# A softplus summed on TensorE instead of VectorE, and four carry columns a slot later, in a convolution and selective-scan kernel

## The reference, cut to what matters

```python
xz = x @ W_in
xh, z = jnp.split(xz, 2, axis=-1)
xh = jax.nn.silu(_causal_conv_k2(xh, conv_w, conv_b))
x_dbl = xh @ W_x
dt_low, Bmat, Cmat = ...                        # 8, 16 and 16 columns
dt = jax.nn.softplus(dt_low @ W_dt + b_dt)      # 256 channels
# per pixel t:  h = exp(dt_t * A) * h + dt_t * B_t * x_t ;  y_t = sum over states (h * C_t)
y = (y + xc * D) * jax.nn.silu(z)
out = y @ W_out
```

## Time and profile before

| | us |
|---|---|
| median of 3 runs (13836.56 to 13845.37) | 13839.43 |
| the profiled execution, its own time | 13837.79 |
| its span, first to last instruction | 13836.0 |
| VectorE busy in it | 13466.6 (97%) |
| GpSimd busy in it | 13246.6 (96%) |
| ScalarE busy in it | 12104.2 (87%) |
| TensorE matmul busy in it | 10079.9 (73%) |

### The profile page before, as it was taken

The page is one execution under the profiler, slowest core; times in us unless marked ns, Lnnn a source line. Parts: engine busy times, 40 slices in busy tenths (PEclk is TensorE's granted clock), DMA queues, the critical chain, the costliest instruction groups (busy, mean ns, idle before and its releaser), DMA issues.

```text
span 13836.0 us, 170380 instructions
## 1 busy us (share of the span) xinstructions
PE 10079.9 (73%) x34752; PEld 2897.7 (21%) x34752; DVE 13466.6 (97%) x12084; ACT 12104.2 (87%) x24809; POOL 13246.6 (96%) x3076
## 2 busy tenths in 40 slices
PE   6777777777777777777777777777777777777776
PEld 1222222222222222222222222222222222222221
DVE  7999999999999999999999999999999999999999
ACT  7888888888888888888988888888898888888888
POOL 6999999999999999999999999999999999999999
PEclk8888888888888888888878888788888888888887
DMA  6667676666766676666667666666666666666665
GB/s 146 161 154 161 155 163 156 158 157 157 164 156 160 152 163 158 160 157 156 158 159 164 153 163 151 163 159 156 161 153 163 156 161 156 160 156 163 158 155 128
DMA packets 1195180, 2175.99 MB, mean 157 GB/s; under 512 B 152321, under 2 KB 161594, under 8 KB 1194042
## 3 DMA queue, kind: packets, MB, share of 16 engines
q1 hardware_dynamic: 1192762, 2164.07, 66.7%
q10 hardware_dynamic: 1280, 0.02, 0.0%
HBM read 1811.17 MB, written 352.32 MB: 156 GB/s over the span
## 4 chain that ended last, share of the span: by engine, by line
POOL 53%; issue 32%; DVE 6%; ACT 5%; PE 1%; DMA 1%; SPq 0%; POOLq 0%; ACTq 0%; DVEq 0%
POOL hq L1064 38%; POOL dbx L1054 15%; DVE hq L946 4%; ACT ps_a L640 2%; DVE dbx L929 1%; ACT dbx L654 1%; DMA b_rep<-bc_d 0%; DMA dt_d<-dt 0%; DVE pp L905 0%; ACT xh L600 0%; ACT L600 0%; ACT L765 0%; PE ps_acc L456 0%; DMA dtx_d<-sp 0%; POOLq L1063 0%
## 5 line engine op out<-in xcount | busy, mean ns | idle before, releaser
L1064 POOL TENSOR_TENSOR hq<-hq,c_rep 128x2048 f32<-128x2048 f32 x2048 | 9251.0, 4535 | 468.8 <-ACT carry L659 465.0
L946 DVE TENSOR_TENSOR_SCAN hq<-ps_a,dbx 128x512 f32<-128x512 f32 x8192 | 9443.6, 1207 | 128.8 <-ACT dbx L654 47.2
L640 ACT ACTIVATE ps_a<-dt_rep,A_neg 128x512 f32<-128x512 f32 x8192 | 5625.2, 687 | 1294.7 <-DVE hq L946 1231.5
L1054 POOL TENSOR_TENSOR dbx<-dtx_rep,b_rep 128x2048 f32<-128x2048 f32 (+1 forms) x1024 | 4082.1, 3986 | 99.1 <-DMA dtx_rep<-dtx_d 89.1
L654 ACT ACTIVATE dbx<-ps_a,dbx,carry 128x1 f32<-128x1 f32 x7168 | 2504.9, 349 | 240.2 <-POOL dbx L1054 140.4
L929 DVE TENSOR_TENSOR dbx<-dtx_rep,ps_b 128x2048 f32<-128x2048 f32 (+1 forms) x1280 | 2626.7, 2052 | 9.5 <-PE ps_b L444 9.3
L456 PE MATMUL ps_acc<-hq,dsum 128*32 128x512 f32 x16384 | 2334.0, 643 | 292.6 <-POOL hq L1064 292.6
L382 PE MATMUL pp<-sq,w_b1T 128*128 128x512 f32 x512 | 531.1, 1141 | 1608.7 <-ACT sq L579 1608.7
L444 PE MATMUL ps_b<-dbl,bsel 41*128 41x512 f32 x2560 | 1587.3, 703 | 153.3 <-DVE dbx L929 97.7
L400 PE MATMUL pp<-x,W_taps 128*128 128x512 f32 x768 | 693.3, 1002 | 895.2 <-DVE x L900 531.4
L456 PEld LDWEIGHTS ps_acc<-hq,dsum 128*32 128x32 f32 x16384 | 355.9, 111 | 1865.7 <-issue 1046.5
(11 more groups left out here) (123 smaller groups left out, 10466.4 us busy)
## 6 DMA issues: line engine op xcount, KB each, us to landing
dtx_rep<-dtx_d SPq DMA_DIRECT2D x2048, 256.0 KB, 5.4
dt_rep<-dt_d SPq DMA_DIRECT2D x2048, 256.0 KB, 6.3
c_rep<-bc_d SPq DMA_DIRECT2D x1024, 256.0 KB, 4.7
xr<-in_x SPq DMA_DIRECT2D x704, 256.0 KB, 10.9
b_rep<-bc_d SPq DMA_DIRECT2D x2048, 64.0 KB, 5.5
dtx_d<-sp SPq DMA_DIRECT2D x256, 512.0 KB, 2.8
dt_d<-dt SPq DMA_DIRECT2D x256, 512.0 KB, 6.1
xin<-in_x SPq DMA_DIRECT2D x256, 256.0 KB, 10.2
```

The costliest lines, as they stand in the source:

```text
L640: A(ps_a[:, BANK[i], :], dt_rep[:, q // NQ, g, :], ACT.Exp, scale=A_neg[:, q // NQ, q % NQ, g:g + 1]).then_inc(exp_done, 1)
L946: v.tensor_tensor_scan(hq[:, q % HQ, g, :], ps_a[:, BANK[i], :], dbx[:, slot(q), g, :], 0.0, ALU.mult, ALU.add).then_inc(scan_done, 1)
L1054: g.tensor_tensor(dbx[:, slot(q), m:, :], dtx_rep[:, d, m:, :], b_rep[:, q % NQ // 2, :].unsqueeze(1).to_broadcast([P, DG - m, T]), ALU.mu ...
L1064: g.tensor_tensor(quad, quad, c_rep[:, c % 2, q % NQ, :].unsqueeze(1).to_broadcast([P, DG, T]), ALU.mult).then_inc(cmul_done, 1)
```

## The change

The log step's sum leaves VectorE. W_dt (with its bias row) is halved once, so that `pp` holds v / 2. The absolute value |v / 2| is kept in `sp`; the exp, with scale -2, and the log go to the buffer `dt`. Two products of TensorE with the identity add `sp` and then `dt` onto `pp`, which then holds v / 2 + |v / 2| + log(1 + exp(-|v|)), the softplus. They stand in slots 12 and 14; the convolution moves to slots 15 to 17, ScalarE's three steps to slots 11 to 13, `pool_part` to slots 14 and 15. VectorE's `softplus` is gone, and `dt_x` waits for TensorE. The wait for the last store of `dt` moves from the copy of slot 17 to the exp. The carry columns of tiles 4, 12, 20 and 28, which are the first of odd quads, move from slot i - 2 to slot i - 1, where they stand ahead of the carry column of tile i + 1.

```diff
-PE_CONV = (11, 12, 13)
+PE_STEP = (12, 14)
+PE_CONV = (15, 16, 17)
-ACT_XZ, ACT_DBL, ACT_SP, ACT_DT, ACT_OUT = 5, 9, (12, 13, 14), 17, 23
+ACT_XZ, ACT_DBL, ACT_SP, ACT_DT, ACT_OUT = 5, 9, (11, 12, 13), 17, 23
...
+IN_BURST = ACT_XZ + 3
+ADD_AT = [[i for i in range(2, NT + 2) if i != IN_BURST and u == (i - 1 if i % (2 * DG) == DG else i - 2)] for u in range(NT)]
...
-POOL_CHUNKS, POOL_SLOTS, ATT_CHUNK = (1, 2, 3, 4), (10, 11), CH - 4
+POOL_CHUNKS, POOL_SLOTS, ATT_CHUNK = (1, 2, 3, 4), (14, 15), CH - 4
...
+            def step_sum(b, c, k):
+                pe.wait_ge(sp_done, 3 * (b * CH + c) + (1, 3)[k])
+                for d in range(DI):
+                    last = mm(pp[:, d, :], w["ident"][:], (sp, dt)[k][:, d, :], start=False, stop=True, skip_group_check=True)
+                if k:
+                    last.then_inc(step_done, 1)
...
                     if k == 1:
-                        A(sp[:], sp[:], ACT.Exp, scale=-1.0).then_inc(sp_done, 1)
+                        if not (isinstance(b, int) and b * CH + c == 0):
+                            act.wait_ge(dt_out, 16 * (b * CH + c))
+                        A(dt[:], sp[:], ACT.Exp, scale=-2.0).then_inc(sp_done, 1)
                     else:
-                        A(sp[:], sp[:], ACT.Ln, bias=1.0).then_inc(sp_done, 1)
+                        A(dt[:], dt[:], ACT.Ln, bias=1.0).then_inc(sp_done, 1)
...
-                    if u + 2 < NT:
-                        if c % CH and u != ACT_XZ + 1:
-                            add_carry(b, c, u + 2)
-                    elif c + 1 < end and (c + 1) % CH:
-                        add_carry(b, c + 1, u + 2 - NT)
+                    for i in ADD_AT[u]:
+                        if i < NT:
+                            if c % CH:
+                                add_carry(b, c, i)
+                        elif c + 1 < end and (c + 1) % CH:
+                            add_carry(b, c + 1, i - NT)
...
+            v.tensor_scalar(w["wdt"][:], w["wdt"][:], 0.5, None, ALU.mult)
...
-            def softplus(b, c):
-                dve.wait_ge(sp_done, 3 * (b * CH + c + 1))
-                v.scalar_tensor_tensor(pp[:, 0:2, :], pp[:, 0:2, :], 0.0, sp[:], ALU.max, ALU.add).then_inc(step_done, 1)
...
                         if u == DVE_DT:
-                            softplus(b, c + 1)
                             dt_x(b, c + 1)
```

More of the change, by code:

```diff
@@ L488, in chunk @@
                             step_dt(b, c + 1)
+                        for k in range(2):
+                            if u == PE_STEP[k]:
+                                step_sum(b, c + 1, k)
                     if c + 2 < end:
@@ L521, in _ @@
             step_dt(0, 0)
+            step_sum(0, 0, 0)
+            step_sum(0, 0, 1)
             for kw in (1, 0, 2):
@@ L677, in evac_dt @@
                 act.wait_ge(dtx_done, b * CH + c + 1)
-                if not (isinstance(b, int) and b * CH + c == 0):
-                    act.wait_ge(dt_out, 16 * (b * CH + c))
                 A(dt[:], pp[:, 0:2, :], ACT.Copy).then_inc(dt_done, 1)
@@ L761, in chunk @@
                         if c % CH:
-                            add_carry(b, c, u + 3)
+                            add_carry(b, c, IN_BURST)
                         silu_z(b, c, 0)
@@ L1017, in _ @@
             add_input(0, 0)
-            softplus(0, 0)
             dt_x(0, 0)
```

## The result

The changed kernel takes 14199.65 us (median of 4 runs, 14198.32 to 14202.19); the kernel before, on the same chip, 13839.46. The ratio is 1.026, 95% interval 1.0242 to 1.0278: **slower, by 360 us**. The prediction was 14050, slower by 211, with a range that ended at 14180. The sign and the way to most of the loss were right; 149 us were missing, and the time lies 20 us outside the range.

The account below looks back on a forecast made before the run. The prediction took VectorE and GpSimd, both nearly full, as the bound. Its chunk terms summed to 6.6 us an image, 211 us over 32 images, on 13837.8: 14049, by the median 14050; range 13850 to 14180.

Parts of the forecast that it names:

- Step 1: VectorE loses L905: 1.22 us in each of 256 chunks, 312.8 in all, counting only if `dt_x` starts sooner.
- Step 2: Way through log and added products to `dt_x`: it starts 0.2 us later, so the 1.22 us are not gained.
- rival D: Added products on TensorE run at the lower clock: up to 1.85 us more in every chunk, 474 us, 14520; chance 0.07.
- Steps 3 and 4: Slots 19 and 27: scans 20 and 28 wait for later carry columns, +0.9 and +0.2 us in a late chunk.
- 2 to 3: Sign of being right: VectorE's waits ahead of `dt_x` and scans 20 and 28, in us a chunk in all.
- Step 5: Slot 3: with tile 4's carry column later, decay 5 goes up to 0.4 us sooner where it waited; late chunks nothing.
- Step 6: ScalarE's absolute value ahead of quad 2's kept column: GpSimd's states 2 wait 1.5 us, chunk 52.8 us.
- GpSimd's ring: Late kept column of quad 2 delays GpSimd's states 2, later work and next chunk's inputs 1, then scan 4: 52.8 us.
- lie side by side: In a late chunk GpSimd's bound, 52.8 us, and VectorE's sum, 52.9 us, are about equally long.
- The sum: Late, second, sixth, seventh chunks +1.3 us each; third, fourth, fifth +0.6 each; first -0.4; 6.6 an image.
- A: `dt_x` 0.5 us or more sooner, carry columns 20 and 28 in time, GpSimd alone bounds: -3.6 an image, 13725; chance 0.08.
- C: Only GpSimd's ring holds, carry columns cost VectorE nothing: 4.2 us an image, 13973; chance 0.20.

Follow-up runs that it names:

- conv_fill: The changed kernel with the first third of the convolution in slot 11, ahead of the first added pair, the rest in slots 15 and 16: 14076.92 us.
- carry_only: The kernel before with only the carry columns of tiles 4, 12, 20 and 28 a slot later: 14191.24 us, ratio 1.0253.
- before_tile4: The kernel before with only the carry column of tile 4 a slot later: 13796.65 us, ratio 0.9972.
- sum_only: The changed kernel with the four carry columns back in their old slots: 14408.25 us, ratio 1.0413.
- the square of four kernels: conv_fill, 14076.92 us; with carry columns 12, 20, 28 back, 14122.62; with quad 2's kept column ahead of the absolute value, 14038.38; with both, 13786.11.
- later_dtx_t4: sum_only with convolution in slots 11-13, added pairs 14-15, softplus steps 12-14, `dt_x` and `dt` copy two slots later, tile 4's carry column one later: 13713.2 us.
- tile4_only: conv_fill with the carry columns of tiles 12, 20 and 28 back in their old slots, only tile 4's a slot later: 14122.62 us, ratio 1.0206.

## Why the prediction was right in the main, and the step that failed

*Step 1, VectorE's work.* Right: L905 is gone, 312.8 us. The busy sum fell by 252.2 only, mostly since the scans' own busy time rose from 9443.6 to 9495.8; the rows don't say why.

*Step 2, the way to `dt_x`.* Right to a tenth where the clock held. By the prediction, counted from the chunk's start (6472.97 there, 6640.88 here), the absolute value would start at 18.6, the log end at 23.3 and `dt_x` start at 25.3. ScalarE and VectorE in the late chunk after:

```profile
6659.42 1.02 ACT L629 ACTIVATE sp<-pp 128x1024 f32<-128x1024 f32 x1 [1.31 <-PE pp L425]
...
6663.08 1.05 ACT L637 ACTIVATE dt<-dt 128x1024 f32<-128x1024 f32 x1
```

```profile
6666.21 1.23 DVE L922 TENSOR_TENSOR sp<-pp,xh 128x1024 f32<-128x1024 f32 x1 [0.58 <-PE pp L384]
...
6671.60 2.34 DVE L959 TENSOR_TENSOR_SCAN hq<-ps_a,dbx 128x512 f32<-128x512 f32 x2 [0.81 <-ACT dbx L671]
...
6684.48 2.34 DVE L959 TENSOR_TENSOR_SCAN hq<-ps_a,dbx 128x512 f32<-128x512 f32 x2 [0.40 <-ACT dbx L671]
```

They give 18.54, 23.25 and 25.33. **The sentence that failed is the one on TensorE: "The first added pair and the sum between them (1 us) are over before the log is."** With 1.98 for the pair it holds; with the 2.7 to 3.8 us of over half of the chunks (3.13 in the third chunk above) it does not, and the second pair starts 138.6 us late in all. I had seen the lower clock in the earlier trace rows and made it rival D, but laid it on the second pair, in every chunk, and gave it 0.07. The rows show the reverse: the second pair runs at full pace in both groups (620 and 618 ns a matmul, after and in conv_fill), the first does not, in 137 chunks of 254. As the first pair had been taken to be hidden, its price stood in neither the sum nor the range. D had the right kind of loss at the wrong pair; its "up to 1.85" is about what the slowest first pairs lose (3.8 against 1.98), but not in every chunk, and in most only in part. Its 474 was far off: the measured price is 123.

The Trainium skill (TensorE: Matmul & The Clock Gate, "HAM oscillation") describes a kernel whose matmul bursts are shorter than the waits between them, and which falls to the lower clock again at every one. The trace shows the same kind of loss where the wait is far the shorter (1.20 us behind 18.5 us of work), and only at 137 of 254 of the waits; conv_fill gives the price.

*Steps 3 and 4, scans 20 and 28.* Right: waits of 0.81 and 0.40 (the two L959 rows above), against 0.9 and 0.4 to 0.5. carry_only has the same two without the sum. Over the run scans 20 and 28 wait 182 and 118 us and `dt_x` 300.1 for TensorE, 2.3 us a chunk, against "2 to 3"; with the scans' other waits for carry columns (450.4 in all) it is 750.5, or 2.9.

*Step 5, tile 4.* Right in size: by itself it makes the third to fifth chunks of the kernel before 0.3 to 0.4 shorter, and the kernel 0.28% or 40 us faster (before_tile4). About 19 of the 40 (an estimate) go with the clock: the row behind the burst is slow in 20 chunks before the change and in none of before_tile4. Without the moved columns the changed kernel loses far more there (sum_only).

*Step 6, GpSimd's ring.* Right in place and time; the wait itself, put at 1.5, is 1.89. GpSimd's states 2 were to start 19.7 us into the late chunk; here is its row, 19.74 in:

```profile
6660.62 4.55 POOL L1075 TENSOR_TENSOR hq<-hq,c_rep 128x2048 f32<-128x2048 f32 x1 [1.89 <-ACT carry L676]
```

That the two bounds "lie side by side", at 52.8 and 52.9, is what the square of four kernels bears out, once its slow rows are taken off.

*The sum, by chunks.* Median length over the images, first to eighth chunk, from one input step to the next:

| | 1st | 2nd | 3rd | 4th | 5th | 6th | 7th | 8th |
|---|---|---|---|---|---|---|---|---|
| before | 61.32 | 51.65 | 52.32 | 52.25 | 54.79 | 52.13 | 51.57 | 51.56 |
| forecast | 60.9 | 52.9 | 52.9 | 52.9 | 55.4 | 53.4 | 52.9 | 52.9 |
| after | 62.08 | 53.01 | 53.85 | 53.19 | 56.62 | 54.27 | 53.11 | 52.99 |
| conv_fill | 60.77 | 52.94 | 52.98 | 52.97 | 55.76 | 53.42 | 53.11 | 52.97 |

The forecast's row is the row of conv_fill, within about 0.2 but for the fifth chunk, which is 0.4 longer in conv_fill. The kernel after departs from it where the first pair is slow: all third chunks +0.9, the fifth +1.2 (+0.9 over conv_fill), the sixth +0.9, the first +1.2, where the forecast was a gain.

*The rivals.* A's condition, that `dt_x` starts in time and the carry columns don't wait, was not met here. In later_dtx_t4, where `dt_x` comes two slots later but hardly waits and the columns of tiles 12, 20 and 28 are in their old slots, the time (13713) is near its 13725, in part by luck: A had the first, third, fourth and fifth chunks shorter, measured are mainly the first, second, third and sixth. The rule of the Trainium skill (Perfetto Trace Analysis, "Identifying the Most-Contended Engine") that the engine of highest occupancy is the one to optimize first points to VectorE; the 13525, with all of L905 off the time, was my reading of it. The measurement differs: with 313 us less on VectorE the kernel is 2.6% slower in one order of the queues and 0.9% faster in the best one tried, as GpSimd is as full. C had the ring right but not alone: with the ring and without the later carry columns of tiles 12, 20 and 28 (tile4_only) the time is 14123, not 13973, or about 14010 without its slow rows.

*What stays open.* Why the clock falls behind a wait of 1.20 us in some chunks and not in others: the waits are of one length, the rows of the late and of the third chunk read alike up to them, and no run bears on that question. The same holds for the row behind the burst, which is slow behind some waits of over 1 us and not behind others.

## What to carry to other kernels

Where two engines are nearly full, look at the order in the queue of a third that serves both: an instruction placed a slot early that must wait there holds up what stands behind it, and the engine it was to help gains nothing. Undo two suspects together as well as one by one, since each alone can look harmless or useless (39 won, 46 lost, 291 together), and compare the clock of the kernels before reading such a difference (the 46 went with a loss of clock). When TensorE gets new work behind a wait, price it at both clocks even where it seems hidden, and see whether work that has to be done anyway can fill the wait.

## What the runs showed of the hardware that I had not expected

- In the third chunk TensorE had worked for 18.5 us with one wait of 1.06 in it, and then waited 1.20 us. Behind that wait the first added pair ran at a clock of 0.61 and took 3.1 us instead of 1.98; over the run it was slow in 137 of 254 chunks. Before the change the only low stretch that I had looked at came after 6.4 us of idling.
- About 1 us of other matmuls in that wait was enough for the first pair to take 1.98 us in all 254 chunks: 123 us, for a change of one line and no change in the work.
- A wait of 1.94 us ahead of a product in sum_only had 7.05 us at a clock of 0.53 behind it, although TensorE was busy throughout; the same row takes 3.89 at full clock. In tile4_only waits of 1.0 to 1.4 us went ahead of 60 slow rows, which are most of what that kernel lost against its expectation.
